# Mamba stage: an explicit table load behind the two SiLU, and the end of the softplus chain one to two states later

## The reference

```python
u = silu(causal_conv(x @ W_in_x.T) + conv_b)
x_dbl = u @ W_x.T
dt = softplus(x_dbl[..., :dt_rank] @ W_dt.T + b_dt)
Bs, Cs = x_dbl[..., dt_rank:dt_rank+16], x_dbl[..., dt_rank+16:]
# for every pixel in order, for 16 states n
h = exp(dt * A) * h + (dt * u) * Bs
y = sum_n h * Cs + u * D_skip
out = (y * silu(z)) @ W_out.T
```

## Time and profile before

| | us |
|---|---|
| median of 3 runs | 7919.82 |
| lowest, highest | 7919.21, 7928.51 |
| profiled execution, its own time | 7927.45 |
| its span | 7925.7 |
| PE, DVE, POOL busy over the span | 5103.3, 4646.6, 4639.4 |
| DVE busy from 4430 to 7840 us | 2997.16 |

### The profile page before, as it was taken

How to read it: one execution, slowest core, us unless ns; L and a number is a source line. 1 busy time by engine, 2 the same in 40 slices (tenths; PEclk the granted TensorE clock), 3 DMA queues, 4 the chain that set the end, 5 groups by cost and what they waited for, 6 DMA issues and landing times. The chain is left out here.

```text
span 7925.7 us, 62957 instructions
## 1 busy us (share of the span) xinstructions
PE 5103.3 (64%) x17178; PEld 2844.4 (36%) x17178; DVE 4646.6 (59%) x4034; ACT 2758.1 (35%) x3950; POOL 4639.4 (59%) x3296
## 2 busy tenths in 40 slices
PE   5962220779655555555554578777777787787787
PEld 2421110224444444444443233333333333333333
DVE  2128887323222222222222588888888888888898
ACT  0000000114200000000000566666666666766665
POOL 0026665000377777777775476776767677767776
PEclk9965555885566767676766899999999999999999
DMA  3013333003333333333332343434343443434343
GB/s 108 10 36 73 73 66 75 33 11 81 92 105 105 113 105 105 114 105 105 113 105 87 113 133 135 139 130 138 125 139 133 130 143 132 131 137 136 131 137 106
DMA packets 371654, 830.33 MB, mean 105 GB/s; under 512 B 193460, under 2 KB 235980, under 8 KB 367448
## 3 DMA queue, kind: packets, MB, share of 16 engines
q1 hardware_dynamic: 286712, 595.95, 25.8%
q0 software_dynamic: 84672, 231.32, 9.8%
HBM read 744.84 MB, written 56.48 MB: 101 GB/s over the span
## 5 line engine op out<-in xcount | busy, mean ns | idle before, releaser
L1052 POOL DMA_INDIRECT sa_quad<-table,sa_idx x1764 | 1668.2, 946 | 1291.4 <-DVE sa_idx L1068 754.4
L1977 POOL TENSOR_TENSOR ma_hc<-ma_h,ma_cc 128x784 f32<-128x784 f32 x1024 | 1890.7, 1847 | 846.4 <-DVE ma_h L1876 747.8
L1539 PE MATMUL ma_bank<-ma_hc,ident 128*128 128x392 f32 x4096 | 1596.3, 513 | 1.8 <-POOL ma_hc L1977 1.8
L1133 PE MATMUL sa_ps<-ident,sa_part 128*128 128x128 f32 (+1 forms) x3920 | 848.9, 410 | 1072.8 <-DVE sa_part L1077 1072.8
L1876 DVE TENSOR_TENSOR_SCAN ma_h<-ma_da,ma_state,ma_bank 128x784 f32<-128x784 f32 x768 | 1416.4, 1844 | 97.2 <-ACT ma_da L1751 38.0
L1077 DVE TENSOR_TENSOR sa_part<-sa_quad,sa_cof 128x2304 f32<-128x2304 f32 x196 | 500.7, 2554 | 1643.2 <-DMA sa_quad<-table,sa_idx 1643.2
L1751 ACT ACTIVATE ma_da<-ma_dt,ma_a_neg 128x784 f32<-128x784 f32 x1024 | 950.6, 944 | 678.5 <-DVE ma_h L1876 672.1
L1133 PEld LDWEIGHTS sa_ps<-ident,sa_part 128*128 128x128 f32 (+1 forms) x3920 | 760.4, 213 | 1135.4 <-DVE sa_part L1077 1090.4
L1864 DVE TENSOR_TENSOR ma_bank<-ma_dtu,ma_bank 128x784 f32<-128x784 f32 x1024 | 979.9, 957 | 30.7 <-PE ma_bank L1526 30.4
L1539 PEld LDWEIGHTS ma_bank<-ma_hc,ident 128*128 128x128 f32 x4096 | 745.5, 200 | 466.2 <-issue 75.7
L1526 PE MATMUL ma_bank<-ma_bc,ma_sel 96*128 96x512 bf16 (+1 forms) x2048 | 542.4, 348 | 446.6 <-DVE ma_h L1876 404.4
(11 more groups left out here) (240 smaller groups left out, 6361.2 us busy)
## 6 DMA issues: line engine op xcount, KB each, us to landing
ma_cc<-c_rows SPq DMA_DIRECT2D x512, 784.0 KB, 4.1
wt_win<-flat SPq DMA_DIRECT2D x64, 878.0 KB, 10.4
sa_quad<-table,sa_idx POOLq DMA_INDIRECT x1764, 2.7
table<-of_xt SPq DMA_DIRECT2D x64, 392.0 KB
ma_xs<-ma_x SPq DMA_DIRECT2D x64, 196.8 KB, 5.3
ma_xs<-ma_x SPq DMA_DIRECT2D x64, 196.5 KB, 5.7
un_xf<-flat SPq DMA_DIRECT2D x8, 816.0 KB
xres<-in_x SPq DMA_DIRECT2D x4, 1568.0 KB, 11.3
```

The costliest lines, as they stand in the source:

```text
L1052: gp.indirect_dma_start(quad[i][:, kk, :], None, k["table"], bass.IndirectOffsetOnAxis(ap=idx[i][:, kk:kk + 1], axis=0))\
L1133: ins = pe.matmul(out, part[e][:, c, taps_r, :], ident[:], start=(c == 0), stop=(c == 3), is_transpose=True)
L1539: ins = pe.matmul(ps_y[:, t, :], ident[:], hc[:, n % RH, at], start=False, stop=(n == DS - 1))
L1977: gp.tensor_tensor(hc[:, i % RH, :], h[:, i % RH, :], cc[:, i % (NGRP * GRP), :], ALU.mult)\
```

## The change

Two things. First, the set that has both Exp and Ln is loaded explicitly behind the two SiLU, in every group and ahead of the first. Second, three steps stand later: `step_size` on DVE moves from slot 10 to slot 12, behind `residue`; `step_product` on POOL from slot 10 to 12; `low_part` from 12 to 13, with the two waits that belong to it.

```diff
@@ act, period
                             silu_gate(G, g)
+                            act.preload_act_table_set("natural_log_exp_and_others")
@@ vector, period
-                        if i == 10 and ready:
-                            step_size(F, 1 - g)
                         if i == 11 and ready:
                             residue(F, 1 - g)
+                        if i == 12 and ready:
+                            step_size(F, 1 - g)
@@ gpsimd, low_part
-                    gp.wait_ge(hcd, START + DS * (F - 1) + 13)
+                    gp.wait_ge(hcd, START + DS * (F - 1) + 14)
@@ gpsimd, period
-                        times_c(G, i, after_low=(F + 1 if i == 13 and ready else ...))
+                        times_c(G, i, after_low=(F + 1 if i == 14 and ready else ...))
-                        if i == 10 and ready:
+                        if i == 12 and ready:
                             step_product(F, 1 - g)
-                        if i == 12 and ready:
+                        if i == 13 and ready:
                             low_part(F, 1 - g)
```

More of the change, by code:

```diff
@@ L1987, in period @@
                     for i in range(DS):
-                        times_c(G, i, after_low=(F + 1 if i == 13 and ready else 1 if i == 0 and older is False else None))
+                        times_c(G, i, after_low=(F + 1 if i == 14 and ready else 1 if i == 0 and older is False else None))
                         if i == 2 and g == 1 and post:
```

## The result

| | us |
|---|---|
| before, median of 4 runs on this chip | 7922.86 |
| after, median of 4 runs (lowest, highest) | 7704.47 (7699.00, 7707.27) |
| after / before | 0.9723, 95% interval 0.9706 to 0.9740 |
| profiled execution after, its span | 7707.27, 7705.5 |

What follows compares the result with a forecast made beforehand. DVE was taken as the bound, its one large gap 3.93 us per group before `step_size`. Loop gain 256.4 plus 2.6 ahead made 259.0 us: 7661 from the 7919.82 median; range 7600 to 7725, the forecast's own 7640 to 7691.

Steps and rivals of the forecast that it cites:

- The large wait: DVE in front of `step_size`, for `correct2` on POOL: 247.5 us in 63 waits, 3.93 a group; forecast to go entirely.
- rival 3: The wait moves to residue because `high_part` comes no earlier; gain 1.8 x 63, 7807 us; chance 0.05.
- waits of 0.4 and 0.6: DVE's residue waits for the copy of `high_part` on ACT, 0.4 us in g = 0 and 0.6 in g = 1.
- So DVE waits for its end, 110.31, and `step_size` ends at 111.15: In g = 0 `step_size`, asked for at 108.92, waits for POOL's `times_c(11)`, started at 108.48, then takes 0.84 us.
- rival 1's second case: `step_size` meets no wait for POOL at all and takes 0.97 us; 7589 us; the whole rival had chance 0.13.
- All of it hidden, price 0: Later `step_product`, `low_part`, next group's decays and loads of C were claimed to cost nothing.
- The slack of 1.4 us: `low_part` ends at 120.2; next group's first `times_b` is due at 122.0, and PE needs 0.4 for its B.
- Rival 5: Slower: `low_part`, two slots later, holds up the next group's B; slower once late by over 5.5 us; chance 0.03.
- 5.7 us ahead of scan 12: Loads of C on SP's queue follow `high_part`'s copy, 5.7 us ahead of scan 12 instead of 7.2; claimed hidden.
- Forecast 256.4: Gain in the Mamba loop: 32 groups at 4.09 us and 31 at 4.05.
- 2.6 us were forecast: Ahead of the first group the table loads at L1701 and L1710 leave the chain, the first hidden behind PE: 2.6 us.
- Rival 2: PE becomes late, busy share rising from 79% to about 85%; a 2.5 us wait in each g = 0, 7741; chance 0.17.

Runs made afterwards that it cites:

- e1_loads_only: Changed kernel with the three steps back in their earlier slots, so only the explicit table load remains; 8335.66 us, 0.9901 of before on the same chip.
- e5_port: Changed kernel with `step_size` made to wait by semaphore for the end of the running `times_c` on POOL; 8327.03 us, 0.9894 of before.
- e4_low_early: Changed kernel with `low_part` one `times_c` earlier, directly behind `step_product`, image loads left in place; 8132.73 us, 0.9652 of before.
- e3_image_late: Changed kernel with the next image's nine pieces issued in four portions behind the next group's rows of C; 8125.31 us, 0.9656 of before.
- e8_low_image: Changed kernel with `low_part` directly behind `step_product` and the next image's pieces issued behind the next group's C rows; 8089.49 us, 0.9576 of before.
- e2_move_only: Changed kernel without the explicit table loads, so only the later steps remain; 8381.64 us, 0.9952 of before on the same chip.
- e9_behind_scan: Changed kernel with `step_size` directly behind scan 11, ahead of `times_b(12)`; 8202.89 us in a single run, 0.974 of before.
- e6_eleven: Changed kernel with `step_size` and `step_product` in slot 11 and `low_part` directly behind `step_product`, ahead of `times_c(12)`; 8175.98 us, 0.9674 of before.
- e7_eleven_image: Changed kernel with `step_size`, `step_product` in slot 11, `low_part` ahead of `times_c(12)`, image pieces behind next group's C rows; 8139.37 us, 0.9638 of before.

## Why the prediction was right, and where its number was off

**Right.** The large wait is gone and not moved (rival 3 falls with the 1.1 us in front of the residue). A load is worth its own 1.28 us and no more (`e1_loads_only`). `b_and_c` ran at full clock (its matmuls took 0.49 us in the median, 0.86 before). At the residue, where waits of 0.4 and 0.6 were forecast, idle times of at most 0.14 us stand in 60 of 64 groups and of 0.21 to 0.32 in the other four.

**The step that mis-sized `step_size`.** "So DVE waits for its end, 110.31, and `step_size` ends at 111.15" is wrong. It took 0.96 us in all groups but the first: rival 1's second case, by the prediction's own bounds 72 us more gain than forecast. The reading of the earlier trace rows was right as to what the length belongs to (`e5_port`), wrong in who yields: a `step_size` that is queued behind a running DVE operation got the access though POOL's operation started 0.62 us before it. POOL's operation was stretched by 1.1 to 1.4 us instead. The prediction also read `scale`'s 2.30 us against 1.84 of its neighbours; alone `scale` takes 1.56 (6266.22 in the trace after).

**"All of it hidden, price 0."** This failed twice.

- *`low_part`.* The slack of 1.4 us was worked out for g = 0. In g = 1 `scale` takes another 1.6 us on POOL, and the 1.4 us of the access are on POOL too. PE waited for `low_part` behind every group with g = 1, DVE up to 1.1 and then again while the clock was low. Price: 75 us in the loop (`e4_low_early`), 34 of them around images. Rival 5 named this mechanism and its direction, but as a case of its own with a chance of 0.03 and a threshold at which it turns the sign; as a cost inside the forecast it stood at nothing.
- *The loads of C.* "5.7 us ahead of scan 12" looked only at the copy that releases SP, not at what stands ahead in SP's queue. Once per image that is the next image, and 14 groups gain nothing. Price: 77.7 us (`e3_image_late`). The trace of before showed it: landing after 19.4 us, POOL idle for 6.11.

**The account of the loop.** Forecast 256.4; plus 72 for `step_size`; less 142.9 for the two together (`e8_low_image` against after), the prices that were put at 0; plus 22, the image's own delay of before (its seven pairs took 778.4 us where 14 groups at 54.0 would take 756), which `e8_low_image` removes too. 256.4 + 72 - 142.9 + 22 = 207.5; measured 206.8. Outside the loop 2.6 us were forecast and 13.5 came: 3.6 ahead of the first group, 9.9 behind the last `step_size`, which the sum does not have. So the point was near by luck: two errors of opposite sign, +72 and -121, partly cancelled, and 11 us outside the loop made the rest look smaller. Rival 2 (PE late, 7741) is nearest in what the profile shows, but its cause, PE's own load, is not the one that was at work: PE was late because `low_part` was, and the low clock it names came behind that wait.

**A faster version.** `e8_low_image` beats both: 0.9576 of before, and 8089.49 / 8230.75 = 0.983 of the changed kernel on the same chip (worked out from the medians; the highest of the one, 8095, is far below the lowest of the other, 8229). Another slot for `scale`, which stands on POOL ahead of `low_part`, was not tried.

## What to carry to other kernels

When a stall goes, all that lay beside it loses its cover: look in the trace of before for every wait on the other engines and queues that ended inside the stall, group by group, the rare groups too (here one image change in eight groups). A slack worked out for one kind of iteration holds for that kind alone; do it for the one with the most work on the engine that is late. And when two engines contend, an operation that gets quicker has a partner that gets slower: look whom the partner feeds.

## What the runs showed of the hardware

**Who gets the shared access.** `step_size` on DVE and a POOL operation, both with two inputs in SBUF, exclude each other. How far POOL's operation had started before `step_size`, in all groups of a trace that had one, and who waited:

| kernel | groups | POOL started earlier by, us | `step_size` | length, us |
|---|---|---|---|---|
| before | 63 | 0.07 to 0.09 | after a semaphore wait | 2.60 |
| `e5_port`, g = 1 | 31 | 0.14 to 0.17 | after a semaphore wait | 2.52 |
| after | 60 | 0.24 to 0.34 and 0.61 to 0.64 | queued behind `times_b` | 0.96, POOL pays |
| `e2_move_only` | 60 | 0.71 | queued behind `times_b` | 0.96, POOL pays, in 59; 1.97 in one |
| `e9_behind_scan` | 63 | 0.86 to 1.31 | queued behind the scan | 1.11 to 1.81 |
| `e6_eleven`, `e7_eleven_image` | 63 each | 0.91 to 1.36 | queued behind the residue | 1.33 to 1.77 |

(In the last three groups of after POOL started 1.74 earlier and was over 0.1 us behind the start of `step_size`, which took 0.96. Three groups of `e2_move_only` with 0.10 to 0.11 look like those of after.) The one group of `e2_move_only` that went the other way, DVE and POOL, and its neighbour:

```profile
8117.32 1.97 DVE L1882 TENSOR_TENSOR ma_dt<-ma_dt,ma_sl 128x784 f32<-128x784 f32 x1
8173.13 0.96 DVE L1882 TENSOR_TENSOR ma_dt<-ma_dt,ma_sl 128x784 f32<-128x784 f32 x1
```

```profile
8116.61 1.84 POOL L1977 TENSOR_TENSOR ma_hc<-ma_h,ma_cc 128x784 f32<-128x784 f32 x1 [1.48 <-DVE ma_h L1876]
8172.42 5.35 POOL L1977 TENSOR_TENSOR ma_hc<-ma_h,ma_cc 128x784 f32<-128x784 f32 x2 [2.23 <-DVE ma_h L1876]
```

Both times POOL starts 0.71 us earlier; once it keeps the access, once it has to give way. The Trainium skill (SBUF — State Buffer, SBUF: two separate sides) says that whichever starts first gets the pair for the whole instruction and the other fully blocks. The exclusion agrees; "starts first" does not by the starts that the profile gives: a queued DVE operation won against POOL operations that had started up to 0.71 us earlier and lost against all those of 0.86 to 1.36. One that is released by a semaphore lost at 0.07. So, counted from POOL's recorded start, a queued `step_size` claims the access some 0.71 us ahead of its own recorded start. Whether POOL claims exactly at its recorded start the profile does not show; the difference between a queued and a released `step_size`, over 0.6 us, does not depend on it. What DVE waits for in that time no run here tells; the simplest form, that it claims when the operation ahead of it starts, falls with `e9_behind_scan`.

**A queue's large transfer.** Rows of C that land 4.1 us after their issue took 17.5 behind nine pieces of an image in the same queue (19.4 in the kernel before).

**A stage that differs between chips.** The same kernel took 7923 us on one chip and 8419 to 8450 on three others, with the Mamba loop within 1.1 us where the changed kernel ran on two. In the profiles the difference lies in one stage, the 1764 indirect gathers on POOL: some 946 ns each everywhere, but they span 2205 us on the first chip and 2691 to 2722 on the others. What they wait for there was not looked into.
